# Where a gate projection is computed: inside a per-sequence loop, or beside the convolution

## The reference, cut to what matters

```
xz = einsum('bld,ed->bel', hidden_states, W_in)      # W_in: 1024 x 256
x, z = split(xz, 2, axis=1)                          # 512 channels each
x = silu(depthwise_conv(x, conv_w) + conv_b)         # 4 taps, causal
k = s4d_kernel(log_dt, log_A_real, A_imag, C_re, C_im, L)
y = irfft(rfft(x, n=2L) * rfft(k, n=2L), n=2L)[..., :L] + x * D
y = y * silu(z)                                      # z: the gate projection
x = layernorm(x_in + einsum('bhl,dh->bld', y, W_out))
```

## Time and profile before

| | us |
|---|---|
| median of 3 runs | 395.71 |
| lowest and highest | 395.20, 395.77 |
| profiled execution, first to last instruction (span) | 390.5 |

### The profile page before, as it was taken

How to read it: one execution, slowest core, us unless ns; L and a number is a source line. 1 busy time by engine, 2 the same in 40 slices (tenths; PEclk the granted TensorE clock), 3 DMA queues, 4 the chain that set the end, 5 groups by cost and what they waited for, 6 DMA issues and landing times.

```text
span 390.5 us, 7319 instructions
## 1 busy us (share of the span) xinstructions
PE 333.8 (85%) x2035; PEld 276.7 (71%) x2036; DVE 249.4 (64%) x491; ACT 124.3 (32%) x332; POOL 225.8 (58%) x390
## 2 busy tenths in 40 slices
PE   2549996789999999999999532799999999999990
PEld 1225544668888887888888422699999999999970
DVE  6997999976887777777776648323443443443431
ACT  2437883541122222222222100144324324334220
POOL 5958994075776767676556502415456556555553
PEclk9957996899999999999999975799999999999996
DMA  7800000243354444444445046401100101001110
GB/s 227 298 0 1 1 0 3 60 136 117 95 155 158 129 151 147 147 134 128 128 128 166 12 176 280 161 2 42 39 29 22 45 27 40 28 20 40 37 37 24
DMA packets 17025, 34.84 MB, mean 89 GB/s; under 512 B 3456, under 2 KB 8455, under 8 KB 16360
## 3 DMA queue, kind: packets, MB, share of 16 engines
q1 hardware_dynamic: 14840, 29.88, 23.8%
q0 software_dynamic: 1872, 4.59, 4.1%
q10 hardware_dynamic: 288, 0.07, 0.1%
HBM read 30.86 MB, written 4.20 MB: 90 GB/s over the span
## 4 chain that ended last, share of the span: by engine, by line
PE 75%; DVE 12%; POOL 4%; issue 4%; ACT 2%; DMA 1%; DVEq 0%; POOLq 0%; ACTq 0%
PE ps L1331 17%; PE ps L1349 15%; PE ps L1200 7%; PE ps L1263 7%; PE ps L1245 6%; PE ps L1147 4%; PE ps L1190 4%; PE ps L1191 4%; PE ps L1283 3%; DVE w L888 2%; DVE w L873 2%; PE ps L1155 1%; PE ps L1287 1%; PE ps L1318 1%; POOL stage_b L583 1%
## 5 line engine op out<-in xcount | busy, mean ns | idle before, releaser
L1331 PEld LDWEIGHTS ps<-stage_b 128*128 128x128 f32 x576 | 68.4, 195 | 2.6 <-DVE stage_b L1096 1.0
L1331 PE MATMUL ps<-stage_b 128*128 128x128 f32 x576 | 68.8, 279 | 1.2 <-ACT stage_b L820 1.2
L1349 PE MATMUL ps<-w,stage_b 128*128 x288 | 65.2, 380 | 0.6 <-DVE stage_b L1121 0.6
L1349 PEld LDWEIGHTS ps<-w,stage_b 128*128 128x128 f32 x288 | 53.3, 190 | 7.5 <-issue 1.0
L603 POOL TENSOR_TENSOR stage_b<-stage_b 112x512 f32<-112x512 f32 x16 | 21.6, 1350 | 42.3 <-DVE stage_b L942 21.7
L925 DVE TENSOR_SCALAR stage_b<-stage_b 112x256 f32<-112x256 f32 (+1 forms) x50 | 20.5, 411 | 35.5 <-POOL stage_b L671 21.8
L811 ACT ACTIVATE stage_b<-ps,b 128x128 f32<-128x128 f32 x144 | 39.2, 384 | 7.2 <-issue 7.2
L942 DVE TENSOR_TENSOR stage_b<-ps,w 112x512 f32<-112x512 f32 x64 | 39.7, 682 | 2.6 <-PE ps L1191 1.3
L643 POOL DMA_INDIRECT stage_b<-x_rows,stage_b x21 | 34.3, 1633 | 10.0 <-issue 6.0
L1200 PEld LDWEIGHTS ps<-w 128*128 128x128 f32 x256 | 32.9, 202 | 8.2 <-issue 6.9
L1096 DVE COPY stage_b<-w 128x2048 f32 x19 | 23.5, 1241 | 19.6 <-issue 14.0
(11 more groups left out here) (156 smaller groups left out, 536.7 us busy)
## 6 DMA issues: line engine op xcount, KB each, us to landing
w<-in_w SPq DMA_DIRECT2D x16, 512.0 KB, 3.9
w<-in_w SPq DMA_DIRECT2D x16, 256.0 KB, 2.9
w<-in_w SPq DMA_DIRECT2D x4, 1024.0 KB, 8.2
stage_b<-in_ctx SPq DMA_DIRECT2D x16, 224.0 KB, 2.9
w<-in_x_t SPq DMA_DIRECT2D x4, 448.0 KB, 5.3
stage_b<-in_x SPq DMA_DIRECT2D x16, 112.0 KB, 2.9
x_rows<-stage_b SPq DMA_DIRECT2D x16, 112.0 KB, 1.9
w<-in_w_in SPq DMA_DIRECT2D x2, 512.0 KB, 6.4
```

The costliest lines, as they stand in the source:

```text
L1331: last_ = m.matmul(ps[:, 2 * par + f // 4, (f % 4) * P:(f % 4 + 1) * P], w1_now[par][:, k, f * P:(f + 1) * P], rows_t[:, par, k * P:(k + 1 ...
L1349: last_ = m.matmul(ps[:, 4 + par, 0:D], h_t[:, par, f * P:(f + 1) * P], w2[:, e, f, :], start=(f == 0), stop=(f == FT - 1))
```

## The change

The gate projection of all 16 sequences is computed in stage 1, in 16 units of 448 columns, as `a_in` is, into banks 6 and 7 by turns. ACT applies the SiLU to each unit (one instruction of 128 x 448) and leaves the result in SBUF, `z_act`, for all 16 sequences. The 8 units of chunks 0 and 1 (`Z_BEFORE = 2`) come after a_in of chunk 0 on PE, ahead of the count matmuls, and right after the sine on ACT, ahead of SiLU number 0. The other 8 follow one by one behind the units of chunks 1 and 2. The chunk loops of PE and ACT are written out. In the sequence loop `gate_input` and its SiLU are gone, and the gating multiply reads `z_act` at the sequence's place. The load of the gate's half of `w_in` moves ahead of the loads of chunks 1 to 3 of x. `prod`, `y_spec` and `gated` move into the space of `hid_t` and `w_in`, which are done with by then (DVE waits for all 16 SiLUs before its loop); `stage_b` grows from 10176 to 12480 words.

```diff
+        front = r.used
         hid_t = r.cut(DT * T).rearrange("p (k t) -> p k t", k=DT)
         w_in = r.cut(DT * 2 * H).rearrange("p (k h) -> p k h", k=DT)
+        front_words = r.used - front
...
+        r = Region(w2_flat[:, front:front + front_words], front_words)
+        prod = r.cut(4 * H, L).rearrange("p (s h) -> p s h", s=4)
+        y_spec = r.cut(2 * H, L).rearrange("p (s h) -> p s h", s=2)
+        gated = two(HT * L)
-        N_B = 10176
+        N_B = 12480
...
-        z_act, gated = two(HT * L), two(HT * L)
+        z_act = r.cut(NB * HT * L)
...
+        Z_BEFORE = 2
...
+            sp.dma_start(w_in[:, :, H:2 * H], ins["w_in"][:, :, H:2 * H]).then_inc(loaded["w_in_z"], 16)
             for c in range(1, NC):
                 load_hid(c)
             sp.dma_start(consts[:, n_early:], ins["consts"][:, n_early:]).then_inc(loaded["consts"], 16)
-            sp.dma_start(w_in[:, :, H:2 * H], ins["w_in"][:, :, H:2 * H]).then_inc(loaded["w_in_z"], 16)
...
+            def a_gate(c, h):
+
+                unit = HT * c + h
+                act.wait_ge(z_ps, unit + 1)
+                a.activation(z_act[:, CB * c * HT * L:CB * (c + 1) * HT * L]
+                             .rearrange("p (b h t) -> p b h t", b=CB, h=HT)[:, :, h, :],
+                             ps[:, 6 + h % 2, 0:CW].rearrange("p (b t) -> p b t", b=CB), ACT.Silu)\
+                 .then_inc(z_set, 1)
...
                     a.activation(theta, theta, ACT.Sin).then_inc(k_sin, 1)
+                    for n in range(HT * Z_BEFORE):
+                        a_gate(n // HT, n % HT)
...
-            with act.Fori(1, NC - 1) as c:
+            for c in range(1, NC):
                 for h in range(HT):
                     a_unit(c, h)
-            for h in range(HT):
-                a_unit(NC - 1, h)
+                    if c - 1 + Z_BEFORE < NC:
+                        a_gate(c - 1 + Z_BEFORE, h)
...
-                b, par, half = seq(pair, q, 0)
-                if b is not None:
-                    act.wait_ge(z_ps, b + 1)
-                    need(act, gate_set, b - 1)
-                    a.activation(z_act[:, par, :], ps[:, 2, 0:HT * L], ACT.Silu).then_inc(z_set, 1)
...
+            dve.wait_ge(z_set, HT * NC)
...
-                    dve.wait_ge(z_set, b + 1)
                     need(dve, out_ps, b - 1)
-                    v.tensor_tensor(gated[:, par, :], ps[:, 3, 0:HT * L], z_act[:, par, :], ALU.mult)\
+                    v.tensor_tensor(gated[:, par, :], ps[:, 3, 0:HT * L], z_act[:, bass.ds(b * HT * L, HT * L)],
+                                    ALU.mult)\
...
+            def a_gate(c, h):
+                unit = HT * c + h
+                need(pe, z_set, unit - 1)
+                for k in range(DT):
+                    last_ = m.matmul(ps[:, 6 + h % 2, 0:CW], w_in[:, k, H + h * P:H + (h + 1) * P],
+                                     hid_t[:, k, c * CW:(c + 1) * CW], start=(k == 0), stop=(k == DT - 1))
+                last_.then_inc(z_ps, 1)
...
+            pe.wait_ge(loaded["w_in_z"], 16)
+            pe.wait_ge(ends_sb, 1)
+            for n in range(HT * Z_BEFORE):
+                if n % HT == 0:
+                    pe.wait_ge(hid_loaded[n // HT], 16)
+                a_gate(n // HT, n % HT)
+            pe.wait_ge(z_set, HT * Z_BEFORE)
 
             pe.wait_ge(hits_set, PT)
...
+            for c in range(Z_BEFORE, NC):
+                pe.wait_ge(hid_loaded[c], 16)
             for c in range(1, NC):
-                pe.wait_ge(hid_loaded[c], 16)
-            with pe.Fori(1, NC) as c:
                 for h in range(HT):
                     a_unit(c, h)
+                    if c - 1 + Z_BEFORE < NC:
+                        a_gate(c - 1 + Z_BEFORE, h)
...
-            def gate_input(pair, q):
-                b, par, half = seq(pair, q, 0)
-                if b is not None:
-                    need(pe, z_set, b)
-                    for h in range(HT):
-                        for k in range(DT):
-                            last_ = m.matmul(ps[:, 2, h * L:(h + 1) * L], w_in[:, k, H + h * P:H + (h + 1) * P],
-                                             hid_t[:, k, bass.ds(b * L, L)], start=(k == 0), stop=(k == DT - 1))
-                    last_.then_inc(z_ps, 1)
```

More of the change, by code:

```diff
@@ L212, in decoder_layer, with two @@
         b2 = shared[:, :].rearrange("p (e d) -> p e d", e=NE)
-        N_B = 10176
+        def two(words, rows=P):
+            return r.cut(2 * words, rows).rearrange("p (r n) -> p r n", r=2)
+        r = Region(w2_flat[:, front:front + front_words], front_words)
[3 more added lines that the diff above has]
+        N_B = 12480
         stage_b = sb("stage_b", [P, N_B])
         r = Region(stage_b, N_B)
[L219 to L223, removed]
-        z_act, gated = two(HT * L), two(HT * L)
+        z_act = r.cut(NB * HT * L)
         x_res, x1, x2_sum, x2, ctx_sb = two(D, L), two(D, L), two(D, L), two(D, L), two(C, L)
@@ L1215, in kernel_spectrum @@
                 last.then_inc(spec_ps, 1)
-            pe.wait_ge(loaded["w_in_z"], 16)
             pe.wait_ge(loaded["consts"], 16)
@@ L1222, in _ @@
             turn_kernel(1)
-            gate_input(0, 0)
             for h in range(1, HT):
@@ L1233, in step @@
                 if not (isinstance(pair, int) and (pair, q) == (0, 0)):
-                    for part in ((gate_input, transform) if isinstance(pair, int) and (pair, q) == (0, 1)
-                                 else (transform, gate_input)):
-                        part(pair, q)
+                    transform(pair, q)
                 b, par, half = seq(pair, q, 1)
```

## The result

The changed kernel takes 408.29 us (median of 4 runs, 406.0 to 410.12), the kernel before 395.45 (4 runs, 393.07 to 395.77). The ratio is 1.032 with a 95% interval of 1.026 to 1.037: slower by 12.8 us. The prediction was 404.9 with a range of 397 to 409. The profiled execution took 408.85 us with a span of 407.0.

What follows compares the result with a forecast made beforehand. PE was taken to bind the later loop steps, 9.08 us against 8.44, with PE and DVE level in stage 1. Terms +15.0, +0.4 and -6.2 gave +9.2 on 395.7: 404.9 us, range 397 to 409.

Steps and rivals of the forecast that it cites:

- rival 3: Stage 1: PE's clock stays low through part 1, 18.1 us instead of 10.7; total 413; chance 0.10.
- Part 1: Stage 1, eight gate units ahead of the counts: the last six take 10.7 us from a cold start; +3.4 us.
- Part 2: Stage 1, eight gate units beside the convolution: PE's unit becomes 3.47 us, stage 1 grows by 11.6 us.
- Part 3: Change of stages: second transform starts 1.3 us earlier, but half clock costs 1.6 more; taken as +0.4 us.
- Part 4: Sequence loop: the DVE and POOL cycle, L958 held in every step, sets steps of 8.44 us; gain 6.2 us.
- rival 2: Loop: L958 goes ahead of L603, so the cycle is 7.80 us; gain 14.0, total 397.1; chance 0.14.
- Rival 1: Loop: PE binds to the end with steps of 7.31 us; gain 19.9, total 391.2; chance 0.07.
- Rival 4: Stage 1: the gates hide in holes, so it grows by only 3.4 us; total 393.3; chance 0.03.

Runs made afterwards that it cites:

- e4: The kernel before with the 16 wide gate units and their SiLUs added in stage 1, results dropped, gate kept in the loop: 408.29 us, ratio to before 1.032.
- e1: The changed kernel with u (L970) computed first in DVE's loop step, ahead of x1, not behind the products: 398.72 us, ratio to before 1.011.
- e5: The changed kernel with three blocks of eight idle products where the removed gate products had stood between the stages: 404.92 us, ratio to before 1.022.
- e3: The kernel before with the gate's matmuls and SiLU left out of the loop and nothing in their place: 391.09 us, ratio to before 0.993.
- e2: The kernel before with u computed first in DVE's loop step: 396.1 us, ratio to before 1.002.
- e6: The changed kernel with gate units 8 to 15 moved from beside the convolution to the change of stages: 396.42 us, ratio to before 1.0001.
- e8: e6 with e1's edit and two blocks of e5's idle products, ahead of the second transform and behind the third: 385.95 us, ratio to before 0.974.

## Why the prediction was right, and what it mis-sized

The time lies in the range and the mechanism is the one forecast, but one term of the sum was far too small. That the range held it was partly luck: 408.29 is just above the forecast's own 402 to 408, and it is below 409 because the range had been drawn up towards rival 3, half clock through all of part 1, which did not occur. A cold start or a cold part 1 means here that its matmuls begin at 1.2 GHz.

**Part 1, right.** Gate 2 started at 21.46 (21.47), the six took 10.98 us (10.7), the last SiLU ended at 33.02 (32.8), the opening a_in of unit 4 ended by 38.73 (38.7). The choice of the cold start fits this execution; e4 and e1 show the other end, 9.29 against the bound of 9.0. The rule of the Trainium skill ("TensorE: Matmul & The Clock Gate", "HAM oscillation — how this bites in real kernels") that a short pause leaves the clock up is thus borne out by some executions of this very pause (e4's, 1.67 us idle) and not by others (the changed kernel's, 2.49 us).

**Part 2, right.** The unit was 3.45 us (3.47), and the opening a_in of chunk 3 ended at 66.30 (66.5). The eight units added (66.30 - 38.73) - (51.50 - 35.28) = 11.4 us (11.6), and the first product came 14.9 us late (15.0).

**Part 3, the step that failed.** It was put at +0.4 with an upper bound of 1.5. The first product to the first statistics took 20.85 us in place of 16.75: +4.1. The step priced one transform at half clock and credited 1.3 us for its earlier start. The transform came as priced, 2.02 and 1.92. But the step ended there, and the engine went on having pauses: PE stood again from 101 to 104 and the following inverse transform and projection ran at 1.2 GHz, 1.7 us more each. The removed gates of the first sequences had filled just these pauses; e5 puts idle work in them and gets the stretch back to 16.67 and 3.4 us of the total. With this term taken out, at 404.92 us, the kernel is where the forecast had put it; that the two agree to the decimal is chance, for e5's own runs spread over 3.9 us.

**Part 4, right in mechanism, somewhat small in size.** L608 was on time and L970 held in every full step, as the 1490 ns median shows; POOL's L588 released x1's normalization. The step was 8.44 in the first two intervals and 8.49 to 8.64 in the hardware loop, where POOL stands idle for 0.54 to 0.69 us before the inverse square root and not 0.49. The 12 intervals took 224.38 - 121.82 = 102.56 us against 101.3: a gain of 5.0 in place of 6.2. e3, which has no addition, shows the same loop (110.41 us against 110.29). The gating multiply, whose new address was taken at nothing, took 0.61 us, before 0.62.

The rule from the Trainium skill ("SBUF — State Buffer", "Who interferes with whom"), that issue order decides who is held, agrees with the kernel before. L958, issued at 98.06, took 0.48 us; POOL's L603, issued 0.17 us behind it, took 1.45, and 1.27 at 123.64, where L958 was done.

```profile
98.23 1.45 POOL L603 TENSOR_TENSOR stage_b<-stage_b 112x512 f32<-112x512 f32 x1 [2.07 <-DVE stage_b L942]
...
123.64 1.27 POOL L603 TENSOR_TENSOR stage_b<-stage_b 112x512 f32<-112x512 f32 x1 [2.00 <-PE ps L1245]
```

e1 takes the instruction away from L608 altogether: 0.48 us, and a step of 7.81 in the mean of the two shown, where rival 2 had put 7.80.

**The sum.** On the profiled span: +14.9 for stage 1, +4.1 for the first steps, -5.3 for the 13 steps, and +2.9 behind the last statistics of x1, where nothing was changed: 16.5 us with rounding, 390.5 to 407.0. The last term isn't the change's. Before's profile took 170.5 us from there to the end, the other nine kernels 171.0 to 174.2, among them e1 and e5, changed kernels too, 171.3 and 171.0. It goes with the granted clock: the same 965 PE instructions kept PE busy for 141.39 us before, at a mean clock of 0.92, and for 144.61 in the changed kernel's profile, at 0.89. Without it 13.7 us are left, and the medians differ by 12.8.

**From span to time.** The prediction laid 5.2 us around the span, by setting one execution's span beside the median of others. That was wrong. In every later execution, those of the kernel before too, the time lies 1.75 to 1.94 us above the span. So the profiled execution of before took about 392.3 us, a little less than any of its 40 timed ones (392.7 to 397.6). The forecast itself added 9.2 to the median and so isn't touched by this, but the reader should not look for 5 us of anything outside the span.

**The rivals.** Rival 1 (PE binds at 7.31) fell with e3: the removal gave 4.9 us, not 19.9. Rival 2 did not occur by itself, e1 made it occur. Rival 3 needs 18.1 us in part 1; 10.98 and 9.29 were seen. Rival 4 fell with the full 3.45 us of every unit.

What stays open: how much the changed kernel's medians owe to the share of its executions with a cold part 1 (1.7 us), since only profiled ones show where the clock was low. Its mean is on record for each run, and the times follow it: 406.0, 407.73, 408.85 and 410.12 us at 0.935, 0.928, 0.925 and 0.917. Why the medians of e3 and e4 don't add up to the whole is open too. And why POOL starts up to 0.2 us later in the hardware loop was not tested.

## What to carry to other kernels

Work taken off the busiest engine gives back only down to the next cycle: read that cycle's period from a stretch of the trace where the engine isn't binding, look in it for an instruction that lasts longer than its twin elsewhere, and try its place in the order, which was worth 8 to 10 us here against 4.9 for the whole removal. Work that is moved has to land in real holes: eight units in a stage where PE and DVE were level cost 11.4 us, and the same eight in PE's waits of the next stage gave 10.2 of them back. And when an engine loses work between two stages, follow its clock through every pause that opens, not the first alone.

## What the hardware showed unexpectedly

A DVE instruction of one column can be held through a whole series of POOL's. L912 (128x1, both inputs in SBUF) took 0.16 us when free and 2.30 in e2, where POOL's products follow one another every 0.69 us; it ended when POOL's last product did, not between two of them. In the profiles of the kernel before and of e3 it ended there too, at 62.89 and 62.84, after 0.54 and 2.21 us.

PE's clock can fall after the work that follows a pause, not only in the pause: in e6 the transform ran at full speed (1.08 us for its first half) behind 3.30 idle us, and what followed it at half.

The pause of part 1 was 1.33 to 1.69 us in four profiled executions, and the six units behind it took 9.29 us in each; it was 1.95 to 2.49 us in three, and they took 10.98. Its length isn't set by hand: its end hangs on ACT, its start on when PE's first products were done. The spread between runs goes with the granted clock. The ten runs of e6 reach from 393.67 us at a mean clock of 0.952 to 399.55 at 0.932. The four of e8, with the pauses between the stages filled, lie within 1.8 us; whether that comes from the filling is not shown by so few.
